# Norms in halves, layer 1 loaded ahead, and the keys of layer 2 turned by the loads instead of by TensorE

## The reference

```
x = x + L0_xattn(_layernorm(x), ctx) ; x = x + L0_ffn(_layernorm(x))
x = x + L1_xattn(ctx, _layernorm(x))      # 2 heads of 64, queries, keys and values from latents and context
x = x + L1_ffn(_layernorm(x))             # 8 experts, the best 2 of them weighted
x = x + L2_xattn(_layernorm(x), ctx)      # 16 heads of 64:
    xn = _ln(x) * s1 + b1 ; cn = _ln(context) * sc + bc      # eps 1e-6; x was normalised before with 1e-5
    q = xn @ Wq ; k, v = split(cn @ Wkv) ; k, v = null row + k, null row + v
    attn = softmax(q k^T / 4) ; out = _ln((attn v) @ Wo)
x = x + L2_ffn(...) ; x = x + L3_xattn(...) ; x = x + L3_ffn(...)
```

## Time and profile before

| | us |
|---|---|
| three runs | 2397.18, 2398.16 (median), 2400.27 |
| the profiled execution | 2396.25 |
| its span, first to last instruction | 2394.5 |

### The profile page before, as it was taken

One profiled execution on the slowest core, in us unless ns is written; L12 is line 12 of the kernel. 1 busy time (PEld: TensorE's weight loads), 2 busy tenths in 40 slices (PEclk: granted clock), 3 DMA queues, 4 the chain that ended last, 5 costly groups with the idle time before them and its releaser, 6 DMA issues. The chain is left out here.

```text
span 2394.5 us, 48823 instructions
## 1 busy us (share of the span) xinstructions
PE 2147.7 (90%) x19446; PEld 1583.1 (66%) x19446; DVE 1443.5 (60%) x3160; ACT 1203.0 (50%) x2251; POOL 608.6 (25%) x233
## 2 busy tenths in 40 slices
PE   6999999637999698799999999999996889999995
PEld 3666666426888554467777777777773456766773
DVE  5677677568888344645544555455434567776775
ACT  5777776304666332244444444444430366767761
POOL 7656554004666200600000000000000063433400
PEclk8999999757999899799999999999997989999996
DMA  6444444012442001200000000000000254444420
GB/s 167 139 143 130 137 128 114 14 51 82 132 124 77 19 27 51 59 17 17 20 31 17 17 23 27 17 17 17 1 1 14 64 155 124 122 139 130 115 62 17
DMA packets 87072, 165.19 MB, mean 69 GB/s; under 512 B 40384, under 2 KB 48624, under 8 KB 86592
## 3 DMA queue, kind: packets, MB, share of 16 engines
q1 hardware_dynamic: 86848, 162.08, 23.5%
HBM read 81.75 MB, written 0.46 MB: 34 GB/s over the span
## 5 line engine op out<-in xcount | busy, mean ns | idle before, releaser
L1534 PEld LDWEIGHTS L2ps<-L2values,L2probsT 125*128 125x128 f32 (+1 forms) x2688 | 317.5, 192 | 50.6 <-issue 49.6
L1515 PE MATMUL L2ps<-L2keys,L2qz 128*128 128x501 f32 x672 | 340.1, 590 | 0.9 <-DVE L2out_bias L1778 0.9
L1534 PE MATMUL L2ps<-L2values,L2probsT 125*128 125x128 f32 (+1 forms) x2688 | 318.4, 275 | 0.0
L1731 DVE CUSTOM_DVE_ANT_0 L2work<-L2ps,L2maskadd,L2big 128x1503 f32<-128x1503 f32 x112 | 199.8, 1783 | 163.2 <-PE L2ps L1515 163.2
L122 POOL TENSOR_TENSOR rstd<-mv,half_neg 112x8 f32<-112x8 f32 x9 | 16.8, 1866 | 983.3 <-DVE mv L138 983.3
L1529 PEld LDWEIGHTS L2ps<-const,L2work 128*126 128x126 f32 x1344 | 163.8, 140 | 116.3 <-issue 64.7
L647 ACT ACTIVATE L3probsT<-L3ps 128x448 f32<-128x448 f32 x384 | 191.8, 547 | 84.9 <-PE L3ps L504 84.7
L647 ACT ACTIVATE L0probsT<-L0ps 128x448 f32<-128x448 f32 x384 | 193.0, 550 | 66.1 <-PE L0ps L504 66.0
L1529 PE MATMUL L2ps<-const,L2work 128*126 128x128 f32 x1344 | 202.2, 273 | 1.6 <-ACT L2work L1655 0.9
L785 DVE TENSOR_REDUCE L0partmax<-L0ps 112x1 f32<-112x1000 f32 x128 | 153.3, 1197 | 72.1 <-PE L0ps L477 71.9
L1646 ACT ACTIVATE L2z<-L2ps,L2rinv 128x128 f32<-128x128 f32 x112 | 41.1, 367 | 304.8 <-PE L2ps L1534 304.8
(11 more groups left out here) (463 smaller groups left out, 4180.3 us busy)
## 6 DMA issues: line engine op xcount, KB each, us to landing
L0key_stack<-L0key_parts SPq DMA_DIRECT2D x192, 187.5 KB
L3key_stack<-L3key_parts SPq DMA_DIRECT2D x192, 187.5 KB
L0ctxT<-in_ctxT SPq DMA_DIRECT2D x16, 750.0 KB, 4.5
L1raw<-in_ctx SPq DMA_DIRECT2D x16, 750.0 KB
L1rawT<-in_ctxT SPq DMA_DIRECT2D x16, 750.0 KB, 6.2
L2raw<-in_ctx SPq DMA_DIRECT2D x16, 750.0 KB
L3ctxT<-in_ctxT SPq DMA_DIRECT2D x16, 750.0 KB, 4.5
L1fw<-in_L_w SPq DMA_DIRECT2D x16, 256.0 KB, 2.9
```

Source lines behind the costliest of these rows:

```text
L1515: last = nc.tensor.matmul(PS[:, 3 * (m % 2) + c, 0:NPR], tile_rows(m), KT[:, m // RT % 2, 500 * c:500 * c + NPR], start=True, stop=True)
L1534: last = nc.tensor.matmul(PS[:, bank, 0:P], PT[0:keys_in(c), i % 2, c, :], V[0:keys_in(c), i // RT % 2, c, :], start=c == 0, stop=c == NCH ...
L1731: nc.vector.tensor_tensor_reduce(SM[:, m % 2, :].rearrange("p (c n) -> p c n", c=3), PS[:, 3 * (m % 2):3 * (m % 2) + 3, 0:NPR], MA[:, m // ...
```

## The change

**Norms in halves.** `ln_pe`, `ln_pool`, `ln_dve` and `ln_turn` work on tiles 0 to 3 and then on 4 to 7, each half with its own count, so that the halves overlap on the engines. Where the reference normalises twice, the second norm is folded into the first (the variance of a normalised row is known: `1.0 + eps[1]`, `eps[0] * eps[1]`), and one pass is left.

**L1a.** Its weights, the context of batches 0 and 1 and their masks are loaded during L0f (`LatentAhead`), which holds those tiles beside its own. The keys and values of batch 0 move behind the projections, those of batch 1 behind the first scores; some copies move from DVE to ACT, and the first exponential stands earlier.

**L2a.** The weights are loaded during L1f and scaled and centred there by GpSimd, which also takes the powers of the context's variances there (`WideAhead`). In the loop:
- the keys of batches 1 to 15 are no longer made by TensorE: SP loads 127 rows of the turned context straight into the key tile, and two more tiles of 127 x 1500, in which each row is the same 1500 means, or the same 1500 scales, read from a scratch in HBM; GpSimd subtracts the one and multiplies by the other. The tile of the scales lies over the folded weights, both are single, and the keys have two slots;
- the output matmul has its operands swapped, so that it comes out turned (no Z units); for this the probabilities are scaled by the reciprocal on DVE before they are transposed.

Two allocations reach over two stages, so there are two more barriers.

```diff
@@ norms
+    for h in range(2):
+        tiles = range(4 * h, 4 * h + 4)
+        dve.wait_ge(s.ln_tok, h + 1)
+        for t in tiles:
+            last = nc.vector.bn_stats(k.stats[:, t, :], src(t))
...
+            last = nc.vector.tensor_scalar(var, var, 1.0 + eps[1], eps[0] * eps[1], ALU.mult, ALU.add)
@@ L0f, SP
             sp.dma_start(b1[:], src["L0_ffn_b1"].partition_broadcast(TT)).then_inc(s.b_loaded, 16)
+            if ahead:
+                ahead.sync(sp)
@@ L1f, GpSimd (for n in 1, 2), and DVE behind the experts 2, 5 and 6
+            nc.gpsimd.tensor_tensor(self.products[:, n - 1], w, self.ROWS[:, 1:2, :].to_broadcast([64, 16, P]), ALU.mult
+            nc.gpsimd.tensor_tensor(w, w, self.ROWS[:, 0:1, :].to_broadcast([64, 16, P]), ALU.mult).then_inc(s.scaled, 1)
+            nc.gpsimd.tensor_tensor(w[:, :, 0:P - 1], w[:, :, 0:P - 1], w[:, :, P - 1:P].to_broadcast([64, 16, P - 1]),
...
+        link(nc.vector.tensor_reduce(self.U[:, n - 1], self.products[:, n - 1], AX.X, ALU.add))
@@ L2a, SP
+            def load_keys(b):
+                if b == 1:
+                    sp.wait_ge(s.slot_ready, 2)
+                    sp.wait_ge(s.q_filled, 2 * H)
+                else:
+                    sp.wait_ge(s.scores_filled, RT * (b - 1))
+                    sp.wait_ge(s.keys_scaled, b - 1)
+                sp.dma_start(KT[0:P - 1, b % 2, 0:S2], src["ctxT"][b][0:P - 1]).then_inc(s.key_parts, 16)
+                for x, to in enumerate((MEAN[0:P - 1], SCALE_OF)):
+                    sp.dma_start(to, scratch[x, b].rearrange("c n -> (c n)").partition_broadcast(P - 1)).then_inc(s.key_parts, 16)
...
             for b in range(2, B):
                 load_context(b)
                 load_mask(b)
+                load_keys(b)
@@ L2a, TensorE
+                    elif m % RT == 0:
+                        pe.wait_ge(s.keys_scaled, m // RT)
...
-                        last = nc.tensor.matmul(PS[:, bank, 0:P], PT[0:keys_in(c), i % 2, c, :], V[0:keys_in(c), i // RT % 2, c, :],
+                        last = nc.tensor.matmul(PS[:, bank, 0:P], V[0:keys_in(c), i // RT % 2, c, :], PT[0:keys_in(c), i % 2, c, :],
@@ L2a, GpSimd
+            for b in range(1, B):
+                pool.wait_ge(s.key_parts, 48 * b)
+                nc.gpsimd.tensor_tensor(KT[0:P - 1, b % 2, 0:S2], KT[0:P - 1, b % 2, 0:S2], MEAN[0:P - 1], ALU.subtract
+                                        ).then_inc(s.keys_moved, 1)
+                pool.wait_ge(s.keys_moved, b)
+                nc.gpsimd.tensor_tensor(KT[0:P - 1, b % 2, 0:S2], KT[0:P - 1, b % 2, 0:S2], SCALE_OF, ALU.mult
+                                        ).then_inc(s.keys_scaled, 1)
@@ L2a, DVE
+            def scale(m):
+                dve.wait_ge(s.exp_done, m + 1)
+                nc.vector.reciprocal(rinv[:, m % 4:m % 4 + 1], ssum[:, m % 4:m % 4 + 1]).then_inc(s.rinv_ready, 1)
+                dve.wait_ge(s.rinv_ready, m + 1)
+                nc.vector.tensor_scalar(PR[:, m % 2, :], PR[:, m % 2, :], rinv[:, m % 4:m % 4 + 1], None, ALU.mult
```

More of the change, by code:

```diff
@@ L98, in ln_pe @@
     nc = k.nc
[L99 to L102, removed]
+    for h in range(2):
+        for t in range(4):
+            last = nc.tensor.transpose(ps[0:TT, h, t * P:(t + 1) * P],
+                                       (k.xT if stream is None else stream)[:, h * HALF + t * TT:h * HALF + (t + 1) * TT], k.ident)
+        last.then_inc(s.ln_tok, 1)
     if feature_major:
@@ L1040, in _ @@
             nc.tensor.matmul(PS[:, 7, 3 * P + 1:3 * P + 2], W[:, 3, :], BV[:], start=True, stop=True).then_inc(s.bias_filled, 1)
-            for what, j in (("K", 0), ("V", 0), ("K", 1), ("V", 1)):
-                unit(what, 0, j)
             ln_turn(pe, k, s, PS)
@@ L1057, in _ @@
             last.then_inc(s.lat_v, 1)
-            for what, j in (("K", 0), ("V", 0), ("K", 1), ("V", 1)):
-                unit(what, 1, j)
             pe.wait_ge(s.vl_ready, 1)
@@ L1071, in _ @@
             scores(0, range(4))
+            for j in range(3):
+                unit("K", 1, j)
+                unit("V", 1, j)
             for n in range(B):
@@ L1327, in _ @@
             last.then_inc(s.lat_done, 1)
-            empty("K", 1, 2)
             empty("T2", 0, 1)
+            maximum(0)
+            for j in range(3):
+                empty("K", 1, j)
             stats(2)
@@ L1332, in _ @@
             for n in range(B):
-                maximum(n)
                 if n:
+                    maximum(n)
                     empty("Z", n - 1, 0)
@@ L1368, in __init__ @@
         for n in range(self.last_step + 1):
-            self.units += [u for u in (self.first(n), self.second(n), self.extra(n), self.third(n), self.output(n)) if u]
+            self.units += [u for u in (self.first(n), self.second(n), self.third(n), self.output(n)) if u]
         self.place = {u[:3]: i for i, u in enumerate(self.units)}
@@ L1589, in _ @@
                     unit(*plan.first(n))
-                ahead = n + 2 < RT * B
-                if ahead:
+                more = n + 2 < RT * B
+                if more:
                     scores(n + 2, 0)
@@ L1594, in _ @@
                     unit(*plan.second(n))
-                if plan.extra(n):
-                    unit(*plan.extra(n))
-                if ahead:
+                if more:
                     scores(n + 2, 1)
@@ L1780, in _ @@
             maximum(1)
+            scale(0)
             for n in range(plan.last_step + 1):
@@ L2242, in _ @@
                 up(e)
+                if ahead and e == 2:
+                    ahead.variances()
+                if ahead and e in (5, 6):
+                    ahead.vector(dve, link, e - 4)
                 gated(e)
@@ L2388, in build @@
         for name in stages:
-            STAGE[name](nc, k, src)
+            if name == "L0f" and "L1a" in stages:
+                with ExitStack() as both:
+                    ahead = LatentAhead(both, nc, src)
+                    bitlinear_ffn(nc, k, src, ahead)
+                    latent_attention(nc, k, src, ahead)
+            elif name == "L1f" and "L2a" in stages:
+                with ExitStack() as both:
+                    ahead = WideAhead(both, nc, k, src)
+                    mixture_ffn(nc, k, src, "L1", 4, False, ahead)
+                    attention_16_wide_heads(nc, k, src, ahead)
+            elif name not in ("L1a", "L2a"):
+                STAGE[name](nc, k, src)
         store(nc, k, out)
 STAGE = {
-    "L2a": attention_16_wide_heads,
-    "L1a": latent_attention,
     "L0f": bitlinear_ffn,
```

400 lines of the change are left out of this document (200 added, 200 removed).

## The result

| | before | after |
|---|---|---|
| median of 4 runs, us | 2397.67 | 3103.07 (3085.95 to 3113.90) |
| profiled execution, us | 2396.25 | 3102.51 |
| its span, us | 2394.5 | 3100.7 |

The kernel is 29% slower: ratio 1.293, 95% interval 1.287 to 1.299. 3078 was predicted, with a range of 3030 to 3200. Its four runs spread by 0.9%, those of before by 0.2%.

A forecast was written before the change was run, and what follows sets the result against it. TensorE was taken to bound the kernel, full in L2a's loop. 2396.25 + 720.7 - 20.4 - 6 - 13.7 + 0.5 (barriers) = 3077 us, stated as 3078 for the median, range 3030 to 3200.

The forecast's parts named there:

- The keys: L2a's loop: three 127-row transfers per batch share one DMA engine, 88 us, and TensorE waits for them; +720.7 us.
- P: Period of one batch in L2a's loop: issue 0.3, start and landing 2.3, transfers 88, GpSimd 5.8; given as 96 us.
- tail: After fifteen periods of L2a's loop, the last batch up to the first output matmul: 61.6 us.
- L2a ahead of its loop: L2a before its loop: scaled weights at hand let folding and queries start earlier; -20.4 us.
- the norms: Norms in halves overlap on the engines in L2f, L1f, L2a's output, L3f and L0f; -13.7 us in all.
- L1a: L1a: the raw context's wait and one norm pass go, the loop keeps its length; -6 us, between -3 and -15.
- L1f: L1f: GpSimd's weight work, estimated at 58 us, fits its idle time; the norm in halves gives -3.1 us.
- The first rival: L2a's loop: the 127 rows are spread, or three engines used, so keys are hidden; 2329 us, chance 0.12.
- Its term for the loop: L2a's loop with keys hidden: -31.6 for K and Z, +2.6 for the first scaling, -0.9 at the end.

The follow-up runs named there:

- e2: The changed kernel with only the keys' own load cut into 112 and 15 rows, the two repeated-row loads left at 127: 2710.75 us, ratio 1.130 to before.
- f5: e3 with every norm on all eight tiles again, counted once, double norms still folded into one pass: 2344.75 us, ratio 0.979 to before.
- f6: e3 with the weights, contexts and masks of L1a loaded at L1a's own start, as before the change: 2320.87 us, ratio 0.969 to before.
- e1: The changed kernel with each of the three 127-row transfers issued as 112 and 15 rows: 2332.21 us, ratio 0.972 to before.
- e3: e1 with GpSimd in L1f starting on L2a's weights only when DVE has made the gate's parts: 2317.98 us, ratio 0.966 to before.

## Why the prediction was right, and where it was not

- **The keys.** The step that decided (127 rows on SP's queue are one engine's work, at the rate read from rows of 125 and 128) held: 0.06 and 26 GB/s. "That it is the same one for all three no row shows" is settled by e2. The terms of P in the prediction add up to 96.4 and not to 96, and with 96.4 the loop would be +726; the period was 97.0. From the issue to GpSimd 90.1 us passed where the terms have 90.6, but the two GpSimd operations took 3.34 each, 6.8 with their gap, where 5.8 was taken; the nearest row of 3.04 was the better bound and still low. Against 96, 15 x 1.0, the first batch (92.2 us to GpSimd's start in place of 90.1) and a tail of 60.3 for 61.6 make +736.7 of +720.7.
- **L2a ahead of the loop** and **the norms**: right to some 2 us (-22.4 for -20.4; the three norms behind the loop -11.5 for -9.2). f5 says that the halves in all are worth 27 to 30 and not 13.7, with 8.8 of it in L2a ahead of the output norm, which the prediction had priced in another term or, in the loop, not at all. L2f took 8.35 us from the first transposes to the gates, for 8.5.
- **L1a**: -10.7 for -6 (the prediction's own rows give -6.7), within its bounds. The first transposes of probabilities came 58.2 us behind the stage's start, for 65; the loop gave 1.4 back. "The wait of 6.97 us for the raw context goes" was right, but with the loads back in L1a (f6) only 1.45 us of it came back.
- **L1f is the step that failed**: "The work on the weights in L1f ... has a stage of 120 us in which GpSimd is idle; gone wrong, some 5 us on the path". GpSimd had the time, but its instructions are not free for DVE beside them. It cost 15.9 us of waiting and 1.8 in matmuls at the lower clock behind it, against a norm 2.8 faster: +15.1 for -3.1. The estimate asked whether GpSimd was free, and not what DVE did meanwhile.
- **The first rival**, 2329 with the loads spread: e1 gave 2332, with the L1f stall, and e3 2318 without. Its term for the loop, -29.9, measured -30.7 in e3 (973.05 to 1723.58). The mechanism priced there was right, only not on this queue. That the total came so close to it is in part luck: e1 had the stall in L1f and gains elsewhere that were larger than forecast.
- The total missed by 25 us: +16 in the loop, +18 in L1f, and -9 in the other stages together. The last cancelled half of L1f's error.

## What to carry to other kernels

Before a load is moved into a loop, count its rows: on SP's queue here a transfer ran on as many engines as the largest divisor of its rows up to 16, so three loads of 127 rows took 90 us from issue to use, and cut into 112 and 15 they took 12 to 13. Cut a load whose rows divide badly, or issue it where it is spread, and read its DMA share first. Work put on GpSimd because it is idle can be paid by DVE, up to one GpSimd instruction per held operation: place it where DVE reads PSUM or cut it into short pieces, and look whether DVE is on the path there.

## What had not been expected of the hardware

- Single issues on SP lasted up to 29.1 us behind transfers of 127 rows, and everything behind them in the queue waited.
- The same 127 rows landed in 5.7 us when GpSimd issued them, on sixteen engines, which at a share of 1.01 moved only 234 GB/s.
- DVE was held for the length of one GpSimd tensor_tensor (4.4 us, or 1.1 in pieces), but not by a power of 4 us over 24 columns.
